# Six of a step's sixteen scans keep their states in PSUM, and the products by C are shared ten to six between GpSimd and VectorE

## The chip, the cores and the metric

The kernel runs on one core of one Trainium2 chip. The metric is the device time of one execution in microseconds (us). The kernel before took 2140.8 us, the median of three executions (2138.98 to 2144.34). Engines: PE is TensorE (PEld its weight loads), DVE is VectorE, ACT is ScalarE, POOL is GpSimd, SP issues most of the DMAs.

## What is computed

A batch of 16 sequences of 256 tokens with 128 features passes through four selective-scan (Mamba) layers, an output projection with a residual and a layer norm, and then a mixture of eight experts (top 2) with another residual and layer norm. The change touches the scan of the four layers alone:

```python
dA = jnp.exp(d_t[:, :, None] * A)
h = dA * h + (d_t * u_t)[:, :, None] * b_t[:, None, :]
y = jnp.einsum('bdn,bn->bd', h, c_t)
```

256 channels (d) have 16 states (n) each. The time axis is a first-order recurrence, which VectorE's tensor_tensor_scan carries out along the free dimension; the products by C and their sum over n follow.

## The kernel before, in words

**Steps, windows, slots.** The 4096 tokens are cut into 8 groups of 512 columns (two sequences each). A step is one layer of one group: 4 x 8 = 32 steps. Every engine's program runs through the same list of windows (`windows`, L290), one a step, and each window through 16 slots. In window s the scan of step s runs, and between its parts the engines prepare step s+1 (projections, softplus, the transposed products of delta and u), finish step s-1 (gate, output projection) and begin the norm of step s+2. The order on each engine is written out by hand in its `window` function; engines meet by semaphores alone.

**What a slot does.** 256 channels x 16 states are 4096 rows, 128 a tile. A slot is two such tiles (u = 0, 1) of 512 columns. m = slot // 4 counts four blocks of states; a block has four slots.
1. The outer products of B and delta u: 16 small instructions a block write the transposed inputs dbu_t[m % 2]; GpSimd makes 8 (`outer`, L455, lines L469 and L472), ScalarE 8 (`outer`, L630, L641). GpSimd's slots get 4, 2, 2 and 0 of them (POOL_SHARE). Those for the next step's first block lie in slots 13, 14 and 15 (POOL_FIRST); the wait for du_t and b_t that goes ahead of them stands in slot 12, where no outer product does, and in front of that slot's product.
2. TensorE transposes them into PSUM (`to_channels`, L1057, L1067), 8 transposes a slot, into dbu_ps[slot % 2]: two buffers of two banks each. They wait for the scan two slots back, which has read that buffer.
3. ScalarE makes the decays exp(delta A) (`exps`, L549, L563), up to four slots ahead of the scans.
4. VectorE scans (`scan`, L822, L829): inputs decay (SBUF) and dbu_ps (PSUM), states into ring[slot % 8] (SBUF).
5. The product by C, in place in the ring: VectorE for even slots, in the slot after (`times_c`, L834, L838), GpSimd for odd slots, in the slot after (`times_c`, L474, L478; that of slot 15 in slot 0 of the next window). Both operands are in SBUF. 8 products each.
6. TensorE sums over the states: `quad` (L1045, L1052), 4 slices of two slots at a time, into y_ps.

**Around it.** TensorE's window function sets the order of its work behind the transposes of a slot: in slots 0 and 1 a half convolution of the next step each (L1080), in slots 1 and 3 the last two quads of the step before, in slot 2 the z projection (L1090), which waits for ScalarE's silus (xc, L574) and is followed by ScalarE's sz (L579), in slot 4 a skip product (L1167), the dbc projection (L1097, copied by ScalarE at L587) and the mean square, in slot 6 the dt projection, in slot 9 the turned B and the output projection, in slot 11 the transposes of du (`turn_du`, L1145), from slot 5 on a quad in each odd slot. ScalarE's softplus ends with sp_l (L610) in its slot 8; VectorE finishes it in slot 8, behind the scan (L860, L864, L868 delta); GpSimd makes du = delta u in slot 10 (L488); TensorE transposes it; ScalarE copies it out as du_t in its slot 14 (L626); then GpSimd and ScalarE make the next step's first outer products. VectorE's gate (L844) multiplies sz by y_ps in slots 2 and 4. SP copies delta for the decays (d_rep) and brings C (c_rep) for the next step.

Semaphores that matter: scan_done counts scans (16 a step), hc_dve and hc_pool count the products (8 a step each), dbut_pool and dbut_act the outer products, quad_done the quads; a scan in an even slot waits until the quads have read the ring buffers that it and the next overwrite.

After the 32 windows the experts run for some 430 us, without scans; the change touches one wait at their start (`up`, L1270).

Of the kernel before, what the change touches and what calls it, by code (L numbers as in the profile page):

```python
# [21 lines left out]
STEPS = LAYERS * GROUPS  # L22
PAIRS = STEPS // 2
KT = DI // 128
# [9 lines left out]
SZ = 3  # L34
POOL_J = 2
EPS = 1e-5

# [28 lines left out]
def build_program(nc, xT, x_rows, norm_w, Win, conv_w, conv_b, Wx, Wdt, bdt, A_log, Dp, Wblk, Wout, bout,  # L66
                  gate_w, w1, w2, out):
    ctx = ExitStack()
    with ctx:
# [232 lines left out]
        def is_last(s):  # L302

            return has(s, 0) and not has(s, 1)

        def has(s, offset):

            return not isinstance(s, int) or 0 <= s + offset < STEPS
# [15 lines left out]
        def _(sp):  # L324
# [42 lines left out]
            def window(s, i, par):  # L367
# [32 lines left out]
                if is_last(s):  # L400
                    sp.wait_ge(skip_done, STEPS)
                    sp.wait_ge(hc_dve, SLOTS // 2 * (STEPS - 1))
                    sp.wait_ge(hc_pool, SLOTS // 2 * (STEPS - 1))
                    for e in range(EXPERTS):
                        sp.dma_start(w2_sb[e], w2[e, :, :].rearrange("(c p) d -> p c d", p=128))\
                            .then_inc(w2_loaded[e // half], 16)
# [22 lines left out]
        def _(pool):  # L429
# [44 lines left out]
            def times_c(s, i, par, slot):  # L474
                if slot == 1:
                    pool.wait_ge(c_loaded[par], 16 * (i + 1))
# [5 lines left out]
            def window(s, i, par):  # L482
                nxt = 1 - par
                for slot in range(SLOTS):
# [9 lines left out]
                    if slot == 0 and has(s, -1) and has(s, 0):  # L494
                        times_c(s - 1, i if par else i - 1, nxt, SLOTS - 1)
                    elif slot % 2 == 0 and slot and has(s, 0):
                        times_c(s, i, par, slot - 1)
# [23 lines left out]
        def _(act):  # L521
# [61 lines left out]
            def copy_dbc(s, par):  # L583
# [5 lines left out]

                wait(act, hc_dve, SLOTS // 2 * (s - 1))  # L590
                wait(act, hc_pool, SLOTS // 2 * (s - 1))
                act.dma_start(c_dram[par, :, :], dbc[RANK + NS:NBC, :]).then_inc(c_stored, 16)
# [198 lines left out]
        def _(dve):  # L791
# [30 lines left out]
            def scan(s, slot):  # L822
# [4 lines left out]
                if slot % 2 == 0:  # L827
                    wait(dve, quad_done, SLOTS // 2 * s + (slot - RING) // 2 + 1)
                nc.vector.tensor_tensor_scan(ring[slot % RING].rearrange("p u t -> p (u t)"),  # L829
                                             decay[slot % DEC].rearrange("p u a t -> p (u a t)"),  # L830
# [3 lines left out]
            def times_c(s, i, par, slot):  # L834
                if slot == 0:
                    dve.wait_ge(c_loaded[par], 16 * (i + 1))
                dve.wait_ge(scan_done, SLOTS * s + slot + 1)
                nc.vector.tensor_tensor(ring[slot % RING], ring[slot % RING],  # L838
                                        c_rep[par][:, slot // PRS, :].unsqueeze(1).broadcast_to([128, 2, TG]),
                                        ALU.mult).then_inc(hc_dve, 1)  # L840
# [5 lines left out]
            def window(s, i, par):  # L846
                for slot in range(SLOTS):
                    if has(s, 0):
                        scan(s, slot)
                        if slot % 2:  # L850
                            times_c(s, i, par, slot - 1)
                    if has(s, -1):
# [186 lines left out]
        def _(pe):  # L1039
# [5 lines left out]
            def quad(s, m, k):  # L1045

                extra = 1 if is_last(s) and m == M - 1 and k == KT - 1 else 0
                pe.wait_ge(hc_dve, SLOTS // 2 * s + 2 * m + k + 1 + extra)
                pe.wait_ge(hc_pool, SLOTS // 2 * s + 2 * m + k + 1 - extra)
                for j in range(Q):  # L1050
# [6 lines left out]
            def to_channels(s, slot):  # L1057

                m, p = slot // PRS, slot % PRS
                if p == 0:  # L1060
                    pe.wait_ge(dbut_pool, POOL_OUTER * (M * s + m + 1))
                    pe.wait_ge(dbut_act, ACT_OUTER * (M * s + m + 1))
                wait(pe, scan_done, SLOTS * s + slot - 1)
                for u in range(2):
# [205 lines left out]
            def up(g, par, e):  # L1270
# [3 lines left out]
                for c in range(FC):  # L1274
                    if is_first(g, e) and c % 2 == 0:

                        pe.wait_ge(scan_done, SLOTS * STEPS - 1 + c // 2)
                    n = FC * EXPERTS * g + FC * e + c
# [77 lines left out]
```

## Time and profile before

| | |
|---|---|
| median of three executions | 2140.8 us |
| the profiled execution, first to last instruction | 2143.5 us |
| TensorE busy, matmuls | 1877.8 us (88%) |
| VectorE busy | 1943.2 us (91%) |
| ScalarE busy | 1683.8 us (79%) |
| GpSimd busy | 1458.1 us (68%) |
| mean granted TensorE clock | 0.948 |

A core's own time is its span: the profiled execution is 2143.5 us long, 0.1% over the median. The last fifth of the span has no GpSimd work to speak of, so the shares say little; what a change in the scan phase is worth has to be read in one window.

### The profile page before, as it was taken

The page shows a single profiled execution, that of the slowest core. Times are in us where ns is not written, and L with a number is a line of the kernel's source. Part 1 is how long each engine was busy: PE and PEld are TensorE (multiplying, and loading weights), DVE is VectorE, ACT ScalarE, POOL GpSimd, SP SyncE. Part 2 cuts the span into 40 slices and gives each one's busy share as a digit, 9 for nine tenths or more (in the row PEclk, how much of TensorE's full clock was granted, in tenths as well). Part 3 has the DMA queues.
Part 4 walks back from the last instruction along what each step waited for, and adds up shares of the span by engine and source line. Part 5 has one row for each costly group of instructions (what it writes and reads, how often), then busy time and mean ns, then how long its engine had stood idle before and what let it go on. Part 6 is the DMA issues. An engine that isn't in the chain of part 4 may idle for free.

```text
span 2143.5 us, 34659 instructions
## 1 busy us (share of the span) xinstructions
PE 1877.8 (88%) x10816; PEld 1183.1 (55%) x10816; DVE 1943.2 (91%) x1826; ACT 1683.8 (79%) x3053; POOL 1458.1 (68%) x1364
## 2 busy tenths in 40 slices
PE   4788888888888888888888888888888799999998
PEld 1444444444444444444444445444444499989998
DVE  3799999999999999999999999999999987767775
ACT  4899999899999998989999999999999433333333
POOL 2688888888888888888888988888889600000000
PEclk9899999999999999999999999999999999999999
DMA  7323232323232323232333333332322200000000
GB/s 241 86 64 79 63 78 62 78 62 78 62 79 63 80 65 79 64 79 65 81 78 73 81 76 79 78 78 62 78 62 72 84 1 11 11 12 11 11 6 11
DMA packets 72786, 138.55 MB, mean 65 GB/s; under 512 B 13072, under 2 KB 31120, under 8 KB 68112
## 3 DMA queue, kind: packets, MB, share of 16 engines
q1 hardware_dynamic: 66320, 119.28, 22.7%
q10 hardware_dynamic: 6400, 18.42, 3.7%
q8 instruction: 39, 0.64, 0.1%
q14 instruction: 27, 0.22, 0.0%
HBM read 63.85 MB, written 7.74 MB: 33 GB/s over the span
## 4 chain that ended last, share of the span: by engine, by line
ACT 27%; PE 26%; POOL 26%; issue 13%; DVE 6%; ACTq 1%; SPq 1%; DMA 1%; POOLq 0%; DVEq 0%
POOL scan L478 12%; POOL scan L472 11%; PE y_ps L1291 11%; ACT decay L563 10%; PE dbu_ps L1266 8%; ACT scan L641 6%; DVE scan L829 3%; POOL scan L469 2%; PE dbu_ps L1067 2%; ACT sp_e L600 2%; ACT delta L601 2%; ACT sp_l L610 2%; PE y_ps L1052 2%; ACT sp_e L605 1%; ACT du_t L626 1%
## 5 line engine op out<-in xcount | busy, mean ns | idle before, releaser
L829 DVE TENSOR_TENSOR_SCAN scan<-decay,dbu_ps 128x1024 f32<-128x1024 f32 x512 | 1154.6, 2274 | 29.8 <-PE dbu_ps L1067 21.9
L1067 PE MATMUL dbu_ps<-ident,scan 128*128 128x128 f32 x4096 | 571.6, 286 | 220.7 <-DVE scan L829 195.9
L478 POOL TENSOR_TENSOR scan<-scan,c_rep 128x1024 f32<-128x1024 f32 x255 | 671.8, 2635 | 130.4 <-ACT du_t L626 66.5
L1067 PEld LDWEIGHTS dbu_ps<-ident,scan 128*128 128x128 f32 x4096 | 482.2, 147 | 500.1 <-DVE scan L829 259.3
L563 ACT ACTIVATE decay<-d_rep,a_cur 128x510 f32<-128x510 f32 x1024 | 668.0, 709 | 54.1 <-POOL scan L478 15.7
L472 POOL TENSOR_SCALAR scan<-du_t,b_t 128x256 f32<-128x256 f32 x896 | 594.8, 679 | 0.0
L641 ACT ACTIVATE scan<-du_t,b_t 128x256 f32<-128x256 f32 x1024 | 445.6, 494 | 1.2
L838 DVE TENSOR_TENSOR scan<-scan,c_rep 128x1024 f32<-128x1024 f32 x257 | 331.0, 1288 | 0.0
L766 ACT ACTIVATE decay<-dbu_ps 128x512 f32<-128x512 f32 x256 | 147.9, 597 | 205.2 <-PE dbu_ps L1266 183.1
L1052 PE MATMUL y_ps<-scan,sel 128*32 128x512 f32 x2048 | 299.8, 661 | 0.0
L1080 PE MATMUL pre_ps<-xn,w_pre 128*128 128x512 f32 x512 | 245.5, 603 | 5.2 <-DVE w_pre L818 5.2
L507 POOL TENSOR_TENSOR sp_e<-sp_e,bout_rep 128x512 f32<-128x512 f32 x8 | 11.2, 1399 | 277.1 <-DMA sp_e<-in_x_rows 277.1
L1266 PE MATMUL dbu_ps<-split_all 128*128 128x512 f32 x768 | 191.3, 400 | 5.8 <-DVE split_all L892 3.5
L1002 DVE TENSOR_TENSOR decay<-decay 128x512 f32<-128x512 f32 x256 | 163.6, 686 | 9.2 <-ACT decay L766 8.1
L1266 PEld LDWEIGHTS dbu_ps<-split_all 128*128 128x128 f32 x768 | 141.1, 190 | 35.2 <-issue 7.7
L989 DVE SCALAR_TENSOR_TENSOR xc<-y_ps,cw,xc 128x128 f32<-128x128 f32 x256 | 72.0, 344 | 95.4 <-PE y_ps L1291 95.4
L1080 PEld LDWEIGHTS pre_ps<-xn,w_pre 128*128 128x128 f32 x512 | 87.8, 191 | 97.4 <-issue 90.6
L488 POOL TENSOR_TENSOR sp_l<-delta,xc 128x1024 f32<-128x1024 f32 x32 | 75.2, 2351 | 81.2 <-DVE delta L868 81.2
L1291 PEld LDWEIGHTS y_ps<-w_pre,decay 128*128 128x128 f32 x1024 | 119.1, 192 | 3.6 <-issue 1.1
L1291 PE MATMUL y_ps<-w_pre,decay 128*128 128x128 f32 x1024 | 119.5, 275 | 0.2 <-DVE decay L1002 0.2
L1291 PEld LDWEIGHTS y_ps<-c_rep,decay 128*128 128x128 f32 x1024 | 118.0, 192 | 1.9
L1291 PE MATMUL y_ps<-c_rep,decay 128*128 128x128 f32 x1024 | 118.1, 275 | 0.0
(110 smaller groups left out, 1648.8 us busy)
## 6 DMA issues: line engine op xcount, KB each, us to landing
d_rep<-delta SPq DMA_DIRECT2D x496, 128.0 KB, 2.9
c_rep<-c_rows SPq DMA_DIRECT2D x32, 1024.0 KB
w_pre<-prepared_weights ACTq DMA_DIRECT2D x15, 866.0 KB, 13.0
prepared_weights<-scan SPq DMA_DIRECT2D x3, 1122.0 KB, 12.9
scan<-in_conv_w SPq DMA_DIRECT2D x4, 512.0 KB, 5.0
w_out<-prepared_weights SPq DMA_DIRECT2D x16, 128.0 KB, 12.5
sp_e<-in_x_rows SPq DMA_DIRECT2D x8, 256.0 KB, 3.2
d_rep<-in_w ACTq DMA_DIRECT2D x2, 1024.0 KB, 6.8
```

The source lines that it names most:

```text
L472: nc.gpsimd.tensor_scalar(dst, src, col, 1.0, ALU.mult, ALU.mult).then_inc(dbut_pool, 1)
L478: nc.gpsimd.tensor_tensor(ring[slot % RING], ring[slot % RING], c_rep[par][:, slot // PRS, :].unsqueeze(1).broadcast_to([128, 2, TG]), ALU ...
L563: last = nc.scalar.activation(decay[slot % DEC][:, u, :, 1:], src[:, :, 1:], ACT.Exp, scale=a_cur[:, b, m:m + 1])
L641: nc.scalar.activation(dbu_t[m % 2][:, j, :, q, :], du_t[par][:, j, :].rearrange("p (b c) -> p b c", b=UNITS), ACT.Copy, scale=b_t[par][:, ...
L829: nc.vector.tensor_tensor_scan(ring[slot % RING].rearrange("p u t -> p (u t)"), decay[slot % DEC].rearrange("p u a t -> p (u a t)"), dbu_p ...
L838: nc.vector.tensor_tensor(ring[slot % RING], ring[slot % RING], c_rep[par][:, slot // PRS, :].unsqueeze(1).broadcast_to([128, 2, TG]), ALU ...
L1002: nc.vector.tensor_tensor(hid[e % 2][:, c, :], hid[e % 2][:, c, :], hid[e % 2][:, c, :], ALU.mult).then_inc(h2_ready, 1)
L1052: last = nc.tensor.matmul(y_ps[k][CH * j:CH * j + CH, :], sel[:, :], ring[slot % RING][:, j % 2, :], start=False, stop=m == M - 1, skip_gr ...
L1067: last = nc.tensor.transpose(dbu_ps[slot % 2][:, u, 128 * j:128 * j + 128], dbu_t[m % 2][:, j, b, :, :].rearrange("p q c -> p (q c)"), ide ...
L1080: tap = nc.tensor.matmul(o, w_pre[:, c0:c0 + 128], xn[:, :, k:k + SEQ], start=k == 0, stop=k == KC - 1, skip_group_check=True)
L1266: last = nc.tensor.matmul(dst, left[l], right[r], start=start and n == 0, stop=stop and n == len(passes) - 1)
L1291: last = nc.tensor.matmul(moe_ps[e % 2][:, DM * j:DM * j + DM], hid[e % 2][:, c, 128 * j:128 * j + 128], w2_sb[e][:, c, :], start=c == 0, ...
```

## The change

DVE_SLOTS = (2, 4, 6, 8, 10, 14). In these six slots the scan writes its states over its own input in dbu_ps, and VectorE makes the product by C in the same slot, right behind the scan, from PSUM and c_rep into the ring. The other ten products (slots 0, 1, 3, 5, 7, 9, 11, 12, 13, 15) are GpSimd's, each in its slot after; those scans still write into the ring. In the last step VectorE also makes the product of slot 15, as before, but with the states in PSUM. The transposes of slot n+2 wait for VectorE's product n where n is one of the six, and for scan n elsewhere. The counts at the other waits are adapted.

```diff
+DVE_SLOTS = (2, 4, 6, 8, 10, 14)
+DVE_C = len(DVE_SLOTS)
+POOL_C = SLOTS - DVE_C
...
+        def by_vector(s, slot):
+
+            return slot in DVE_SLOTS or is_last(s) and slot == SLOTS - 1
+
+        def vector_products(s, slot):
+
+            return DVE_C * s + sum(by_vector(s, n) for n in range(slot + 1))
+
+        def pool_products(s, slot):
+
+            return POOL_C * s + sum(not by_vector(s, n) for n in range(slot + 1))
...
-                    sp.wait_ge(hc_dve, SLOTS // 2 * (STEPS - 1))
-                    sp.wait_ge(hc_pool, SLOTS // 2 * (STEPS - 1))
+                    sp.wait_ge(hc_dve, DVE_C * (STEPS - 1))
+                    sp.wait_ge(hc_pool, POOL_C * (STEPS - 1))
...
             def times_c(s, i, par, slot):
-                if slot == 1:
+                if slot == 0:
                     pool.wait_ge(c_loaded[par], 16 * (i + 1))
...
-                    elif slot % 2 == 0 and slot and has(s, 0):
+                    elif slot and has(s, 0) and not by_vector(s, slot - 1):
                         times_c(s, i, par, slot - 1)
...
-                wait(act, hc_dve, SLOTS // 2 * (s - 1))
-                wait(act, hc_pool, SLOTS // 2 * (s - 1))
+                wait(act, hc_dve, DVE_C * (s - 1))
+                wait(act, hc_pool, POOL_C * (s - 1))
...
-                nc.vector.tensor_tensor_scan(ring[slot % RING].rearrange("p u t -> p (u t)"),
+                states = dbu_ps[slot % 2][:, :, :] if by_vector(s, slot) else ring[slot % RING]
+                nc.vector.tensor_tensor_scan(states.rearrange("p u t -> p (u t)"),
...
-                if slot == 0:
+
+                if slot == DVE_SLOTS[0]:
                     dve.wait_ge(c_loaded[par], 16 * (i + 1))
                 dve.wait_ge(scan_done, SLOTS * s + slot + 1)
-                nc.vector.tensor_tensor(ring[slot % RING], ring[slot % RING],
+                nc.vector.tensor_tensor(ring[slot % RING], dbu_ps[slot % 2][:, :, :],
...
-                        if slot % 2:
-                            times_c(s, i, par, slot - 1)
+                        if slot in DVE_SLOTS:
+                            times_c(s, i, par, slot)
...
-                extra = 1 if is_last(s) and m == M - 1 and k == KT - 1 else 0
-                pe.wait_ge(hc_dve, SLOTS // 2 * s + 2 * m + k + 1 + extra)
-                pe.wait_ge(hc_pool, SLOTS // 2 * s + 2 * m + k + 1 - extra)
+                wait(pe, hc_dve, vector_products(s, PRS * m + 2 * k + 1))
+                wait(pe, hc_pool, pool_products(s, PRS * m + 2 * k + 1))
...
-                wait(pe, scan_done, SLOTS * s + slot - 1)
+                back, before = (s, slot - 2) if slot >= 2 else (s - 1, slot - 2 + SLOTS)
+                if has(s, -1) or slot >= 2:
+                    if by_vector(back, before):
+                        pe.wait_ge(hc_dve, vector_products(back, before))
+                    else:
+                        pe.wait_ge(scan_done, SLOTS * back + before + 1)
...
-                        pe.wait_ge(scan_done, SLOTS * STEPS - 1 + c // 2)
+                        last = SLOTS - 2 + c // 2
+                        if by_vector(STEPS - 1, last):
+                            pe.wait_ge(hc_dve, vector_products(STEPS - 1, last))
+                        else:
+                            pe.wait_ge(scan_done, SLOTS * (STEPS - 1) + last + 1)
```

## Rows read from the trace of the kernel before

**Rows 1.** The page: busy time of the engines; VectorE's product; the delta line, all windows

```profile
PE 1877.8 (88%) x10816; PEld 1183.1 (55%) x10816; DVE 1943.2 (91%) x1826; ACT 1683.8 (79%) x3053; POOL 1458.1 (68%) x1364
...
L838 DVE TENSOR_TENSOR scan<-scan,c_rep 128x1024 f32<-128x1024 f32 x257 | 331.0, 1288 | 0.0
...
L868 DVE TENSOR_TENSOR delta<-delta,sp_l x32: 1224/1225/1382, 40.8 to 1635.3; 128x1024 f32<-128x1024 f32 x32
```

**Rows 2.** Four stretches of one window: length; PE, PEld, DVE, ACT, POOL busy (instructions); clock; DMA

```profile
780.21:790.09 9.88, 9.88 (x52) 5.67 (x52) 9.87 (x7) 7.29 (x13) 9.88 (x10) 1.00 0.00 0
790.09:809.04 18.95, 18.59 (x105) 9.56 (x104) 17.88 (x11) 18.04 (x29) 17.38 (x18) 1.00 0.15 40
809.04:821.92 12.88, 8.16 (x50) 5.12 (x48) 12.78 (x8) 12.18 (x24) 8.19 (x6) 0.87 0.93 197
821.92:831.54 9.62, 7.71 (x42) 3.42 (x40) 9.62 (x6) 6.39 (x14) 9.46 (x11) 1.00 0.41 94
```

**Rows 3.** Timeline, TensorE's transposes 0 and 2, VectorE's scan 2 (start, length)

```profile
780.21 1.09 PE L1067 MATMUL dbu_ps<-ident,scan 128*128 128x128 f32 x8 [0.56 <-POOL scan L472]
...
786.54 1.09 PE L1067 MATMUL dbu_ps<-ident,scan 128*128 128x128 f32 x8
...
787.75 2.29 DVE L829 TENSOR_TENSOR_SCAN scan<-decay,dbu_ps 128x1024 f32<-128x1024 f32 x1
```

**Rows 4.** Waits of the whole run: us in total, times, longest

```profile
POOL scan L478 <- ACT du_t L626: 66.5, 31, 2.5
...
PE dbu_ps L1067 <- POOL scan L472: 20.8, 31, 2.8
```

**Rows 5.** Timeline of GpSimd behind du_t, in two windows, and TensorE's transposes 0'

```profile
770.10 2.92 POOL L478 TENSOR_TENSOR scan<-scan,c_rep 128x1024 f32<-128x1024 f32 x1 [1.65 <-ACT du_t L626]
...
822.08 2.37 POOL L478 TENSOR_TENSOR scan<-scan,c_rep 128x1024 f32<-128x1024 f32 x1 [2.43 <-ACT du_t L626]
...
824.39 0.62 POOL L469 TENSOR_TENSOR scan<-du_t,b_t 128x256 f32<-128x256 f32 x1
...
824.99 3.31 POOL L472 TENSOR_SCALAR scan<-du_t,b_t 128x256 f32<-128x256 f32 x5
...
831.68 1.09 PE L1067 MATMUL dbu_ps<-ident,scan 128*128 128x128 f32 x8 [0.81 <-POOL scan L472]
```

**Rows 6.** Timeline of VectorE beside it: product 12, scans 14 and 15, scans 0' and 1'

```profile
826.31 1.20 DVE L838 TENSOR_TENSOR scan<-scan,c_rep 128x1024 f32<-128x1024 f32 x1
827.42 4.45 DVE L829 TENSOR_TENSOR_SCAN scan<-decay,dbu_ps 128x1024 f32<-128x1024 f32 x2
...
833.13 4.55 DVE L829 TENSOR_TENSOR_SCAN scan<-decay,dbu_ps 128x1024 f32<-128x1024 f32 x2
```

**Rows 7.** Timeline of softplus on VectorE, of TensorE's transposes of du, of ScalarE's du_t

```profile
809.07 1.25 DVE L860 SCALAR_TENSOR_TENSOR sp_w<-sp_w,sp_e 128x1024 f32<-128x1024 f32 x1 [0.72 <-ACT sp_l L610]
810.36 1.38 DVE L864 SCALAR_TENSOR_TENSOR sp_l<-sp_l,sp_w 128x1024 f32<-128x1024 f32 x1
...
818.38 1.56 PE L1145 MATMUL pre_ps<-ident,sp_l 128*128 128x128 f32 x8
...
820.86 1.06 ACT L626 ACTIVATE du_t<-pre_ps 128x512 f32<-128x512 f32 x2
```

**Rows 8.** Timeline: a GpSimd product beside VectorE's, outer products beside a gate

```profile
845.79 3.25 POOL L478 TENSOR_TENSOR scan<-scan,c_rep 128x1024 f32<-128x1024 f32 x1 [0.35 <-DVE scan L829]
...
848.93 0.66 DVE L844 TENSOR_TENSOR sz<-sz,y_ps 128x512 f32 x1
...
849.02 1.84 POOL L472 TENSOR_SCALAR scan<-du_t,b_t 128x256 f32<-128x256 f32 x4
```

**Rows 9.** Timeline: TensorE's transposes 4, ScalarE's dbc copy, ScalarE's decays 0'

```profile
791.15 1.09 PE L1067 MATMUL dbu_ps<-ident,scan 128*128 128x128 f32 x8
...
794.99 0.59 ACT L587 ACTIVATE dbc<-pre_ps 96x512 f32<-96x512 f32 x1 [0.24 <-PE pre_ps L1097]
...
828.88 1.33 ACT L563 ACTIVATE decay<-d_rep,a_cur 128x510 f32<-128x510 f32 x2 [3.20 <-DMA d_rep<-delta]
```

## The prediction

> **What bounds the kernel now.** I read the page first, then cut one window of the scan phase at the points where one engine hands over to the next, and then read the timelines at those points. A window is one of the 32 steps (16 slots each); scan n, product n and transposes n are those of slot n, and a dash marks the next window. The delta row [rows 1] runs from 40.8 to 1635.3 us over 32 windows, so a window takes 51.4 us. VectorE is busy 91% of the span [rows 1], and in the four stretches of a whole window 9.87 + 17.88 + 12.78 + 9.62 = 50.1 of 51.3 us [rows 2]. That looks like a VectorE bound, and a change that takes two products away from VectorE looks like a gain.
>
> The same rows show a second loop that is just as long. It goes from the start of TensorE's transposes 0 to the start of transposes 0', in four legs that follow each other without a gap [rows 2]:
> - 9.88 us on TensorE: transposes 0, half a convolution, transposes 1, the other half, a quad, transposes 2, then the z projection; ScalarE's second sz ends the leg. TensorE is busy 9.88 of 9.88 us. VectorE's scan 2 starts at 787.75, when transposes 2 have just ended [rows 3].
> - 18.95 us on ScalarE, to the end of its sp_l; busy 18.04.
> - 12.88 us on ScalarE, to the end of the du_t copies; busy 12.18.
> - 9.62 us on GpSimd (busy 9.46), to the last outer product for m = 0, on which transposes 0' wait.
>
> The waits confirm the two hand-overs of the last leg: in 31 windows GpSimd's product waits for du_t, and in 31 TensorE's transposes wait for GpSimd's outer product [rows 4]. GpSimd is idle much of the window (busy 68% of the span [rows 1]), but this leg is full. So the loop through TensorE, ScalarE and GpSimd and the VectorE loop are within about half a microsecond of each other: transposes 0' started at 831.68 [rows 5], scan 0' at 833.13 [rows 6], 1.45 us later. Where a scan waits for its transposes it starts 1.2 us behind their start (786.54 and 787.75 [rows 3]), so GpSimd's leg has 0.2 us of slack to VectorE here.
>
> **The change, part by part.**
> 1. *VectorE loses products 0 and 12.* A product lasts 1.29 us in the mean [rows 1] and overlaps with what follows by 0.09 (826.31 + 1.20 against 827.42 [rows 6]), so 2 x 1.2 = 2.4 us of VectorE work per window go. A product now directly follows its own scan and waits for it: by the softplus pair, which also waits for its predecessor (809.07 + 1.25 to 810.36 [rows 7]), such a start comes 0.04 us after the end, where the product's successor overlapped by 0.09. That is 0.13 us six times, 0.8 us back. VectorE's work becomes 50.1 - 2.4 + 0.8 = 48.5 us.
> 2. *The lock between VectorE and GpSimd goes.* A GpSimd product beside a VectorE product of two SBUF operands takes 3.25 us in place of 2.36 [rows 5, 8]. Beside the gate (848.93, one operand in PSUM, one in SBUF) four outer products take 1.84 us, 0.46 each, undisturbed [rows 8]. The new product has exactly the gate's kinds of operands, so I take no block at all; the other bound is the old 1.0 us each. The Trainium skill, SBUF — State Buffer, section "SBUF: two separate sides", gives the same reason: VectorE with two SBUF inputs and GpSimd take one shared port pair exclusively; the trace agrees by the rows just named.
> 3. *GpSimd gains products 0 and 12.* Product 0 comes in GpSimd's slot 1, behind the last leg; the outer products behind it (m = 1, needed by transposes 4, 10.9 us after transposes 0 [rows 3, 9]) would be done after: outer products 2.0, product 15 2.3, two outers 0.9, product 0 2.3, two outers 0.9, together 8.4 us. It is hidden, with 2.5 us left. Product 12 comes in slot 13. GpSimd's slot 12 holds the wait for du_t, even though no outer product stands there, and product 11 behind it; then four outers, now product 12, two outers, product 13, two outers, and only then transposes 0' may start. So product 12 lies whole on the fourth leg: +2.32 us (a product's pitch, 822.08 to 824.39 [rows 5]). The leg without blocks is 0.16 + 2.32 + 0.60 + 5 x 0.46 + 2.32 + 2 x 0.46 = 8.6 us [rows 5, 8]; with product 12 it is 10.9. Before it was 9.62, because VectorE's product 12 at 826.31 [rows 6] stretched the five outers to 3.31; in the window ahead product 11 was hit too (2.92 us [rows 5]). Net: +1.3 us in the one kind, +0.9 in the other.
> 4. *Transposes n+2 now wait for product n where n is VectorE's.* TensorE starts transposes 4 at 791.15 [rows 9]. Scan 2 ends at 790.04 [rows 3], product 2 follows and ends 1.2 later, so transposes 4 start at about 791.35: +0.2. Queued behind them are the skip, the dbc projection and the mean square, and ScalarE already waits 0.24 for dbc [rows 9], so the 0.2 goes into the loop. At the other five the wait is covered: TensorE comes to the later transposes behind its own fillers, when the product is over on my walk of the window; product 14 releases transposes 0', which GpSimd holds longer.
> 5. *Softplus comes behind product 8.* VectorE now idles 0.72 us for sp_l there [rows 7]; the product takes 1.2, so delta comes about 0.4 later. du goes through GpSimd and TensorE's transposes back to ScalarE, which in this kind of window reaches du_t only at 820.86, 0.9 us after the transposes' end at 818.38 + 1.56 [rows 7]; in every other window (no DMA issue and self-wait on ScalarE) TensorE is last, and the 0.4 counts. Mean +0.2.
> 6. *Scans write in place into PSUM.* No row shows VectorE writing PSUM. Nearest is the gate, which reads there. I take no difference; if each of the six cost up to 0.1 us more, it would lie in the idle time of step 7. Below nothing I see no reason for a gain. A product from PSUM I take as 1.2, too. The Trainium skill, VectorE: DVE Perf Modes, section on the TRN2 errata, speaks against the change: a fixed 120 cycles for a PSUM source against 58, some 65 ns at its clock. The gate row (0.66 us for 512 elements) shows no such term. By the page product 2 would end 0.07 later and the loop be 0.07 longer, some 2 us in all.
> 7. *The sum.* 2.32 - 1.1 (blocks gone, mean of the two kinds) + 0.2 + 0.2 = +1.6 us per window; where d_rep comes late, as by 3.20 us at 828.88 [rows 9], the longer leg hides part of it, so I take +1.4. Over 31 windows that is +44 us. VectorE gets 48.5 us of work in a window of 52.9 and idles mostly before scans 0' and 2. The changed waits ahead of the c_rows store and ahead of the w2 loads are met long before; the first up projections of the second stage wait for a product in place of a scan, once, at most 1.2 us.
>
> The profiled execution took 2143.5 us, the median is 2140.8, 0.1% less; I add the 44 us to the median: **2185 us**. A measurement of this kernel tells about 0.3% (6.4 us) from no change.
>
> **The rivals.**
> - *VectorE was the true bound (faster).* If product 12 did not lengthen GpSimd's leg, because du_t comes early enough or the leg has more room than 0.2 us, the loop could fall to ScalarE's: its 51.3 less the 1.1 of blocks, plus 0.4, about 50.6, or -0.7 us x 31 = -22: 2119 us. It decides at a fourth leg under 9.3 us. For it speaks VectorE's 91%; against it that rows 4 count 31 windows of 31. Chance 0.08.
> - *Blocks stay, or PSUM is slow.* If the product on PSUM still locks GpSimd out, product 14 falls beside products 12 and 13 and adds 1.0 us per window: 2216 us. The same comes of in-place scans that are 1 us longer each (6 us on 48.5 pass the loop). The gate row speaks against the first; nothing shows the second. Chance 0.14.
> - *A draw.* GpSimd's leg grows by 0.9 only and steps 4 and 5 cost nothing, and late d_rep is hidden: +0.3 us or less a window, under 2150 us. Chance 0.08, half of it within 0.3%.
> - *My forecast:* 0.70.
>
> **The numbers.** Steps 4 and 5 at nothing and 0.9 for GpSimd give +28, 2169; step 5 whole in all windows and 1.3 everywhere give +59, 2200. I reach down to 2158 for part of the draw and up to 2216 for the lock. Faster 0.09, same 0.05, slower 0.86.
>
> **What would show it.** GpSimd's leg, du_t's end to the last outer for m = 0, near 10.9 us with product 12 at 2.36; outer products at 0.47 us and products at 2.36 everywhere outside softplus; VectorE's busy time down by about 80 us, and its idle time ahead of scans, put down to the transposes L1067, up by about 100. GpSimd's busy time falls although it has 64 products more in all. The forecast is wrong if scan 0' still starts behind VectorE's own work, if the first leg is no longer 9.9 us, or if the in-place scans exceed 2.4 us.

## The result, and the profile after

The kernel after takes 2224.51 us (median of 4 runs, 2223.39 to 2225.40), the kernel before 2141.61 us on the same chip (4 runs, 2138.98 to 2144.34). The ratio is 1.0381, 95% interval 1.0361 to 1.0402: slower by 83 us, where 44 us were forecast. The direction held, the size did not: 2224.5 lies above the range, which ended at 2216. The profiled execution took 2225.26 us, its span 2223.5.

From the page of the kernel after: busy time, share of the span and number of instructions of each engine; then the share of each engine in the chain that ended last; then the groups of instructions that answer to [rows 1, 6, 8] (busy time, mean ns of one | idle time ahead of them, and what ended it). Scans are now L845, VectorE's products L855, GpSimd's products L493 and outer products L487, the transposes L1088, the convolution L1101.

```profile
PE 1908.3 (86%) x10816; PEld 1185.6 (53%) x10816; DVE 1865.4 (84%) x1762; ACT 1681.5 (76%) x3053; POOL 1359.1 (61%) x1428
...
PE 36%; ACT 26%; issue 12%; POOL 9%; DVE 8%; ACTq 1%; DMA 0%; POOLq 0%; SPq 0%; DVEq 0%
...
L493 POOL TENSOR_TENSOR scan<-scan,c_rep 128x1024 f32<-128x1024 f32 x319 | 754.6, 2366 | 223.9 <-DVE scan L845 139.9
L845 DVE TENSOR_TENSOR_SCAN scan<-decay,dbu_ps 128x1024 f32<-128x1024 f32 x319 | 724.0, 2279 | 138.1 <-PE dbu_ps L1088 136.3
...
L845 DVE TENSOR_TENSOR_SCAN dbu_ps<-decay,dbu_ps 128x1024 f32<-128x1024 f32 x193 | 439.7, 2278 | 58.2 <-PE dbu_ps L1088 49.2
...
L487 POOL TENSOR_SCALAR scan<-du_t,b_t 128x256 f32<-128x256 f32 x896 | 417.8, 483 | 0.0
...
L1101 PE MATMUL pre_ps<-xn,w_pre 128*128 128x512 f32 x512 | 280.1, 676 | 6.0 <-DVE w_pre L833 5.7
L855 DVE TENSOR_TENSOR scan<-dbu_ps,c_rep 128x1024 f32<-128x1024 f32 x193 | 236.3, 1225 | 8.8
```

Most of the local prices are as forecast. VectorE's busy time fell by 77.8 us (about 80 were expected). A scan in place in PSUM costs 2278 ns, one into SBUF 2279; a product from PSUM costs 1225 ns. GpSimd's products are at 2366 ns and its outer products at 483, so the lock is gone, and GpSimd's busy time fell by 99 us although it has 64 products more. VectorE waits 185 us for the transposes (136.3 + 49.2), 164 more than before (21.9), where some 100 more were expected.

One line of this page is not as forecast: the 512 convolution matmuls take 280 us together, 35 more than before (245.5), though nothing in them was changed. The stretches of one window show why. As in [rows 2], a line is a stretch: its length, busy us of PE, PEld, DVE, ACT, POOL, the granted clock and the DMA. The first line is leg 1 of a window in which the clock did not fall; the second is the idle stretch ahead of the transposes 0 of another window, and the other four are legs 1 to 4 of that window.

```profile
921.51:931.39 9.88, 9.88 (x52) 5.67 (x52) 6.87 (x3) 6.34 (x11) 9.88 (x11) 1.00 0.00 0
...
1026.44:1028.51 2.07, 0.02 (x2) 0.01 (x1) 1.18 (x1) 2.07 (x6) 2.07 (x4) 1.00 0.00 0
1028.51:1040.08 11.57, 11.57 (x52) 6.53 (x52) 6.87 (x3) 6.30 (x11) 10.57 (x11) 0.85 0.00 0
1040.08:1059.33 19.25, 17.56 (x102) 8.99 (x101) 18.78 (x12) 18.03 (x29) 14.93 (x18) 1.00 0.15 37
1059.33:1072.22 12.89, 9.14 (x52) 5.62 (x51) 12.69 (x9) 12.18 (x24) 5.70 (x5) 0.87 0.95 194
1072.22:1083.19 10.97, 7.91 (x43) 3.51 (x41) 9.34 (x5) 10.29 (x21) 10.82 (x12) 1.00 0.36 89
```

Legs 2 to 4 are 19.25, 12.89 and 10.97 us; the working of the prediction had 19.15, 12.88 for this kind of window and 10.9. Leg 1 is 11.57 us in place of 9.88, with the same 52 matmuls, TensorE busy all through, at a granted clock of 0.85. Ahead of it TensorE had done 0.02 us of work in 2.07.

The timelines of TensorE and VectorE around three starts of leg 1 (start, length, in brackets the idle time ahead and what ended it). The first pair is the window in which the clock did not fall.

```profile
921.51 1.09 PE L1088 MATMUL dbu_ps<-ident,scan 128*128 128x128 f32 x8 [2.02 <-POOL scan L487]
922.44 1.88 PE L1101 MATMUL pre_ps<-xn,w_pre 128*128 128x512 f32 x4
...
1028.51 1.52 PE L1088 MATMUL dbu_ps<-ident,scan 128*128 128x128 f32 x8 [2.05 <-POOL scan L487]
1029.82 3.18 PE L1101 MATMUL pre_ps<-xn,w_pre 128*128 128x512 f32 x4
...
1083.32 1.71 PE L1088 MATMUL dbu_ps<-ident,scan 128*128 128x128 f32 x8 [2.89 <-POOL scan L487]
1084.83 2.98 PE L1101 MATMUL pre_ps<-xn,w_pre 128*128 128x512 f32 x4
1085.17 2.29 DVE L845 TENSOR_TENSOR_SCAN scan<-decay,dbu_ps 128x1024 f32<-128x1024 f32 x1 [3.58 <-PE dbu_ps L1088]
```

TensorE stands idle for 1.9 to 3.1 us ahead of transposes 0', 2.4 in the mean. Before it was 0.2 to 0.8 ([rows 3] and [rows 5] show 0.56 and 0.81). Of the 30 windows that follow another and have a whole leg 1, in 25 the granted clock then falls to its lower level, 1.2 GHz, at some point between 0.3 us before the start of the transposes and 1.3 us behind it, and leg 1 lasts 11.4 to 11.6 us; in five the clock stays at 2.4 GHz and leg 1 lasts 9.8 to 9.9. Four convolution matmuls take 3.18 us in the one case, 1.88 in the other. VectorE idles 3.58 us ahead of scan 0', for TensorE's transposes, which wait for GpSimd. The wait of the transposes for GpSimd's outer product, in us over the whole run, times and longest, against the second line of [rows 4]:

```profile
PE dbu_ps L1088 <- POOL scan L487: 77.0, 32, 4.4
```

It is 56 us longer than before, about 1.8 us a window.

GpSimd behind du_t, in the window whose legs stand above, against [rows 5]:

```profile
1072.37 2.38 POOL L493 TENSOR_TENSOR scan<-scan,c_rep 128x1024 f32<-128x1024 f32 x1 [3.13 <-ACT du_t L641]
1074.71 0.62 POOL L484 TENSOR_TENSOR scan<-du_t,b_t 128x256 f32<-128x256 f32 x1
1075.30 1.40 POOL L487 TENSOR_SCALAR scan<-du_t,b_t 128x256 f32<-128x256 f32 x3
1076.66 2.39 POOL L493 TENSOR_TENSOR scan<-scan,c_rep 128x1024 f32<-128x1024 f32 x1
1079.00 0.96 POOL L487 TENSOR_SCALAR scan<-du_t,b_t 128x256 f32<-128x256 f32 x2
1079.90 2.37 POOL L493 TENSOR_TENSOR scan<-scan,c_rep 128x1024 f32<-128x1024 f32 x1
1082.24 0.95 POOL L487 TENSOR_SCALAR scan<-du_t,b_t 128x256 f32<-128x256 f32 x2
```

The product at 1076.66 is the added one, product 12. Nothing is blocked any more, every duration is the short one, and the leg is still 1.2 us longer on the mean.

The account in us, as means over 25 windows in the middle of the scan phase (numbers 3 to 27, counted from 0). A window is its four legs and 0.14 us between the last outer product and transposes 0'.

| part of the window | before | after | forecast |
|---|---|---|---|
| leg 1, TensorE | 10.01 (9.88, but 11.6 in two, at full clock, d_rep late) | 11.34 (11.4 to 11.6, but 9.88 in three) | 9.88 |
| leg 2, ScalarE | 18.95 | 19.26 | 19.15 |
| leg 3, ScalarE | 12.6 | 12.5 | 12.8 |
| leg 4, GpSimd | 9.76 | 10.97 | 10.9 |
| window | 51.49 | 54.17 | 52.9 |

Legs 2 to 4 add 1.36 us together (+0.31, -0.16, +1.21), close to the forecast's 1.4. The other half of the loss, 1.33 us a window, came with leg 1.

### The profile page after: what moved, and what is told of

Read it like the earlier page. It is cut to its first block, busy times and chain, and to the rows that moved or that the text cites. A ratio compares the mean times of both kernels' runs of the same rounds, so it can differ in the third digit from the quotient of the medians.

```text
span 2223.5 us, 34532 instructions
## 1 busy us (share of the span) xinstructions
PE 1908.3 (86%) x10816; PEld 1185.6 (53%) x10816; DVE 1865.4 (84%) x1762; ACT 1681.5 (76%) x3053; POOL 1359.1 (61%) x1428
## 3 DMA queue, kind: packets, MB, share of 16 engines
q1 hardware_dynamic: 66320, 119.28, 21.9%
## 4 chain that ended last, share of the span: by engine, by line
PE 36%; ACT 26%; issue 12%; POOL 9%; DVE 8%; ACTq 1%; DMA 0%; POOLq 0%; SPq 0%; DVEq 0%
PE y_ps L1316 10%; ACT decay L578 10%; PE dbu_ps L1287 8%; ACT scan L656 6%; PE dbu_ps L1088 6%; PE pre_ps L1101 6%; POOL scan L487 4%; DVE dbu_ps L845 4%; POOL scan L493 4%; PE pre_ps L1118 2%; DVE scan L855 2%; PE y_ps L1068 2%; ACT sp_e L615 1%; ACT delta L616 1%; DVE scan L845 1%
## 5 line engine op out<-in xcount | busy, mean ns | idle before, releaser
L493 POOL TENSOR_TENSOR scan<-scan,c_rep 128x1024 f32<-128x1024 f32 x319 | 754.6, 2366 | 223.9 <-DVE scan L845 139.9
L845 DVE TENSOR_TENSOR_SCAN scan<-decay,dbu_ps 128x1024 f32<-128x1024 f32 x319 | 724.0, 2279 | 138.1 <-PE dbu_ps L1088 136.3
L1088 PE MATMUL dbu_ps<-ident,scan 128*128 128x128 f32 x4096 | 570.7, 284 | 274.0 <-DVE scan L845 164.2
L1088 PEld LDWEIGHTS dbu_ps<-ident,scan 128*128 128x128 f32 x4096 | 475.9, 145 | 571.6 <-DVE scan L845 251.8
L845 DVE TENSOR_TENSOR_SCAN dbu_ps<-decay,dbu_ps 128x1024 f32<-128x1024 f32 x193 | 439.7, 2278 | 58.2 <-PE dbu_ps L1088 49.2
L487 POOL TENSOR_SCALAR scan<-du_t,b_t 128x256 f32<-128x256 f32 x896 | 417.8, 483 | 0.0
L1101 PE MATMUL pre_ps<-xn,w_pre 128*128 128x512 f32 x512 | 280.1, 676 | 6.0 <-DVE w_pre L833 5.7
L855 DVE TENSOR_TENSOR scan<-dbu_ps,c_rep 128x1024 f32<-128x1024 f32 x193 | 236.3, 1225 | 8.8
L1101 PEld LDWEIGHTS pre_ps<-xn,w_pre 128*128 128x128 f32 x512 | 99.9, 216 | 111.9 <-issue 104.1
```

Of the source, the lines that this page charges most:

```text
L487: nc.gpsimd.tensor_scalar(dst, src, col, 1.0, ALU.mult, ALU.mult).then_inc(dbut_pool, 1)
L493: nc.gpsimd.tensor_tensor(ring[slot % RING], ring[slot % RING], c_rep[par][:, slot // PRS, :].unsqueeze(1).broadcast_to([128, 2, TG]), ALU ...
L845: nc.vector.tensor_tensor_scan(states.rearrange("p u t -> p (u t)"), decay[slot % DEC].rearrange("p u a t -> p (u a t)"), dbu_ps[slot % 2] ...
L855: nc.vector.tensor_tensor(ring[slot % RING], dbu_ps[slot % 2][:, :, :], c_rep[par][:, slot // PRS, :].unsqueeze(1).broadcast_to([128, 2, TG]),
L1088: last = nc.tensor.transpose(dbu_ps[slot % 2][:, u, 128 * j:128 * j + 128], dbu_t[m % 2][:, j, b, :, :].rearrange("p q c -> p (q c)"), ide ...
L1101: tap = nc.tensor.matmul(o, w_pre[:, c0:c0 + 128], xn[:, :, k:k + SEQ], start=k == 0, stop=k == KC - 1, skip_group_check=True)
```

## The experiments

The account that is tested has two parts: product 12 lies on GpSimd's leg and makes everything behind it 1.4 us later, as forecast; and the longer wait ahead of transposes 0' leaves TensorE without work, upon which its clock falls and leg 1 costs 1.7 us more. Against it stood that the states in PSUM are what costs, that ten products are too many for GpSimd wherever they lie, and that leg 1 waits for late products. Each expectation names the theories that its own run decides between, so "theory 2" isn't the same one everywhere. Each run was compared with the kernel before on the same chip; its median was 2144.06 us for runs 1 to 4, 2142.17 for runs 5 to 8 and 2143.49 for runs 9 to 11.

**1. Keep TensorE awake.** The kernel after, with 14 spare transposes of the identity into the bank that transposes 0' overwrite, done while TensorE waits for the outer products.

```
                 if slot == 0 and has(s, -1):
                     for n in range(14):
                         nc.tensor.transpose(dbu_ps[0][:, 0, 0:128], ident[:, :], ident[:, :])
                 if p == 0:
                     pe.wait_ge(dbut_pool, POOL_OUTER * (M * s + m + 1))
                     pe.wait_ge(dbut_act, ACT_OUTER * (M * s + m + 1))
```

> Changed kernel, but in slot 0 TensorE first makes 14 spare transposes of the identity into the dbu_ps buffer that it is about to overwrite, in the time in which it waits for GpSimd's outer products (2.1 to 2.9 us idle). Theory 1 (clock): the second half of the loss comes from TensorE's granted clock, which falls to its lower level behind that idle time in 27 of 31 windows and makes the first leg 11.56 us in place of 9.88. Then the leg is 9.88 in nearly all windows and the time 2224.5 - 27 x 1.7 = about 2179 us. Theory 2 (late product): the first leg is longer because a wait stands in it (a quad or a convolution waits for the later products 12 and 13); spare transposes change nothing, 2224 us or a little more.

Measured: 2188.10 us, ratio 1.0212 (1.0192 to 1.0231). The timeline of TensorE in one window of it, then the stretch of leg 1:

```profile
1005.89 1.69 PE L1084 MATMUL dbu_ps<-ident 128*128 128x128 f32 x14
...
1008.00 1.09 PE L1091 MATMUL dbu_ps<-ident,scan 128*128 128x128 f32 x8 [0.42 <-POOL scan L487]
1008.93 1.88 PE L1104 MATMUL pre_ps<-xn,w_pre 128*128 128x512 f32 x4
```

```profile
1008.00:1017.88 9.88, 9.88 (x52) 5.67 (x52) 6.87 (x3) 6.42 (x11) 9.88 (x11) 1.00 0.00 0
```

More work on TensorE makes the kernel 36 us faster. Transposes 0' still wait for the last outer product, leg 4 is still 10.97 us, but the clock is at its upper level in leg 1 of all 30 windows, leg 1 is 9.88 in all but two of the middle ones (10.24 and 10.72), and the window 52.89 us. What remains against the kernel before is 2188.10 - 2144.06 = 44.0 us. So the loss of 83 us has two parts, each by itself on the chip: some 36 us of clock, and 44 us of the longer loop (the three medians were taken apart, which leaves 2 or 3 us between the two parts and the whole). The time is 9 us above the expected 2179. In part the expectation counted 27 windows with a low clock, where the trace has 25. In part the edit has a cost of its own: it also puts the waits for the outer products behind the wait for the product two slots back, transposes 4 now start 0.24 us behind the end of VectorE's product 2 in place of 0.05, and leg 2 is 19.42 in place of 19.25. At 0.17 us a window that is some 5 us, so the clock's share is nearer 41 us and that of the longer loop nearer 39.

**2. Give product 12 back, and move product 8 to GpSimd instead.** The same split of six and ten, one constant changed.

```
-DVE_SLOTS = (2, 4, 6, 8, 10, 14)
+DVE_SLOTS = (2, 4, 6, 10, 12, 14)
```

> Changed kernel with products 2, 4, 6, 10, 12, 14 on VectorE (12 in place of 8), so product 12 leaves the part of GpSimd's work between du_t and the outer products for m = 0, and product 8 goes to GpSimd's slot 9, where it waits for delta anyway. Theory 1 (product 12 on GpSimd's leg is the cause, and the clock follows from it): GpSimd's leg 8.6 us in place of 10.97, first leg 9.88, window 50.4 us, time 2141 - 31 = about 2110 us, faster than both. Theory 2 (ten products are too many for GpSimd wherever they are): 2200 us or more. Theory 3 (VectorE holds the end of the window as soon as GpSimd does not): 2130 to 2145 us.

Measured: 2214.48 us, ratio 1.0327 (1.0310 to 1.0344); a miss. Leg 4 falls to 9.5 us (theory 1 wanted 8.6; in it GpSimd waits for scan 13, 0.68 us in one window), leg 1 is 9.82 at the full clock, and yet the window is 53.77. GpSimd's product 8 now falls beside softplus. The timeline of this kernel there, VectorE, GpSimd, TensorE:

```profile
625.45 3.43 DVE L877 SCALAR_TENSOR_TENSOR sp_w<-sp_w,sp_e 128x1024 f32<-128x1024 f32 x1 [0.73 <-ACT sp_l L625]
625.45 2.35 POOL L493 TENSOR_TENSOR scan<-scan,c_rep 128x1024 f32<-128x1024 f32 x1
...
633.66 1.97 PE L1088 MATMUL dbu_ps<-ident,scan 128*128 128x128 f32 x8 [5.44 <-DVE scan L845]
635.55 1.94 PE L1068 MATMUL y_ps<-scan,sel 128*32 128x512 f32 x8
```

Softplus's first instruction takes 3.43 us where it took 1.25 [rows 7]: this time it is VectorE that is held for as long as GpSimd's product lasts, and GpSimd that is undisturbed. Delta ends 6.0 us behind sp_l in place of 4.2 in the kernel after, TensorE idles 5.44 us ahead of transposes 11, which take 1.97 us for 1.09, and leg 3 becomes 14.3 us. Transposes 0' come another 0.9 us behind the last outer product. A new place of the lock and a low clock in another leg took back most of what legs 1 and 4 gained. The time also lies in the range of theory 2, ten products being too many anywhere. Run 7 decides between the two.

**3. The states back in SBUF, all else as after.**

```
-                states = dbu_ps[slot % 2][:, :, :] if by_vector(s, slot) else ring[slot % RING]
+                states = ring[slot % RING]
...
-                nc.vector.tensor_tensor(ring[slot % RING], dbu_ps[slot % 2][:, :, :],
+                nc.vector.tensor_tensor(ring[slot % RING], ring[slot % RING],
```

> Changed kernel with the states of all scans in the ring in SBUF, and VectorE's products from there; split, order and waits as in the changed kernel. Theory 1 (VectorE's two SBUF operands lock GpSimd out, PSUM states take that away): GpSimd's products beside VectorE's take 3.25 us again, product 14 adds 1.0 us to GpSimd's leg (12.0 us), the time is 2224 + 31 = about 2255 us. Theory 2 (PSUM states are themselves dear, in-place scans or products from PSUM are slower): the time falls below 2220 us.

Measured: 2352.25 us, ratio 1.0974 (1.0955 to 1.0992), 128 us slower than after. The groups of its page that answer to those above, and one of VectorE's products from its timeline:

```profile
L855 DVE TENSOR_TENSOR scan<-scan,c_rep 128x1024 f32<-128x1024 f32 x193 | 302.1, 1565 | 8.9
...
L487 POOL TENSOR_SCALAR scan<-du_t,b_t 128x256 f32<-128x256 f32 x896 | 567.0, 646 | 0.0
```

```profile
736.99 2.35 DVE L855 TENSOR_TENSOR scan<-scan,c_rep 128x1024 f32<-128x1024 f32 x1
```

The lock is back in both directions: outer products 646 ns in place of 483, VectorE's products 1565 in place of 1225, 33 of the 193 at 2.34 us or more. The direction is theory 1's; the size is four times what it said. Leg 4 is 13.03 us, so transposes 0' come later still, and TensorE idles 3.15 us ahead of them. Its clock is low from 0.9 us before their start to 5.9 us behind it, and leg 1 takes 12.78 us:

```profile
637.47:650.25 12.78, 12.78 (x52) 7.41 (x52) 6.86 (x3) 4.50 (x7) 10.59 (x11) 0.77 0.00 0
```

Theory 2 falls: putting the states into PSUM is the good part of this change. At this split it saves 128 us.

**4. Product 12 off the leg.** The kernel after, with products 12 and 13 behind the last outer products for m = 0, in GpSimd's slot 15.

```
+                    elif slot == SLOTS - 1 and has(s, 0):
+                        for late in (SLOTS - 4, SLOTS - 3):
+                            times_c(s, i, par, late)
-                    elif slot and has(s, 0) and not by_vector(s, slot - 1):
+                    elif slot and has(s, 0) and slot < SLOTS - 3 and not by_vector(s, slot - 1):
```

> Changed kernel, but GpSimd makes products 12 and 13 in its slot 15, behind the last outer products for m = 0. GpSimd's leg from du_t to the last of these becomes 6.3 us. Theory 1: the window is then set by VectorE up to product 14, which releases TensorE's transposes 0': about 49.3 to 50.5 us, 2075 to 2115 us, and the clock stays at its upper level ahead of them. Theory 2 (the late products hold the quads in TensorE's slots 1 and 3, or the outer products for m = 1 come too late for transposes 4): 2130 us or more.

Measured: 2134.57 us, ratio 0.9954 (0.9940 to 0.9968). Leg 4 is 6.30 us, the window 51.28. It is faster than the kernel before, but 20 us above the range of theory 1 and inside that of theory 2. The reasons that theory 2 gave are not the cause, though: leg 1 is 9.82 and leg 2 19.25 us in most windows, so neither quads nor transposes 4 are held. The timeline shows what comes next:

```profile
604.29 1.97 PE L1091 MATMUL dbu_ps<-ident,scan 128*128 128x128 f32 x8 [3.67 <-DVE scan L848]
...
608.05 1.97 PE L1169 MATMUL pre_ps<-ident,sp_l 128*128 128x128 f32 x8
...
611.16 4.46 DVE L848 TENSOR_TENSOR_SCAN scan<-decay,dbu_ps 128x1024 f32<-128x1024 f32 x2 [1.29 <-PE dbu_ps L1091]
```

Here it is transposes 11 that TensorE reaches too early: it waits 3.67 us for scan 9, which VectorE does behind softplus, and does them and the transposes of du at the low clock (1.97 us for 1.09). VectorE then waits 1.29 us ahead of scan 12.

**5. The same move in the kernel before.** Product 13 alone behind the outer products; states in SBUF, eight and eight.

```
-                    elif slot % 2 == 0 and slot and has(s, 0):
+                    elif slot % 2 == 0 and 0 < slot < SLOTS - 2 and has(s, 0):
                         times_c(s, i, par, slot - 1)
+                    elif slot == SLOTS - 1 and has(s, 0):
+                        times_c(s, i, par, SLOTS - 3)
```

> Kernel before, but GpSimd makes product 13 in its slot 15, behind the last outer products for m = 0, so its leg from du_t to these falls from 9.8 to about 7.4 us. Theory 1 (two loops of the same length before the change: GpSimd's and VectorE's): VectorE holds the window then, the gain is at most 0.3 us a window, 2135 to 2144 us, no difference that can be told. Theory 2 (GpSimd's loop alone was the bound and VectorE followed): 2144 - 31 x 2.3 = about 2072 us.

Measured: 2126.21 us, ratio 0.9920 (0.9891 to 0.9949), a gain of 16 us and 9 us under the range of theory 1. Leg 4 falls by 2.2 us to 7.52, the window only by 0.6, to 50.9. VectorE then idles 0.9 us in it (1.35 before), 0.64 of it for sp_l and 0.12 for transposes. That is the prediction's reading of the kernel before: two loops within about half a microsecond of each other. Even so, half a microsecond a window was open to a reordering of GpSimd's queue alone.

**6. The PSUM part alone.** Eight products stay on each engine, the even ones on VectorE from PSUM.

```
-DVE_SLOTS = (2, 4, 6, 8, 10, 14)
+DVE_SLOTS = (0, 2, 4, 6, 8, 10, 12, 14)
```

(and GpSimd's wait for the replicated C is back in slot 1, its first product.)

> The PSUM part of the change alone: products 0, 2, 4, ..., 14 on VectorE from states in PSUM, each right behind its scan, the other eight on GpSimd as before. Theory 1: GpSimd's leg is 8.6 us without blocks, VectorE's work 51 us a window is the bound, 2125 to 2150 us: the loss of the whole change comes from the two products more on GpSimd. Theory 2: the PSUM part itself costs (the transposes' wait for the product, the product's wait for its scan): 2165 us or more.

Measured: 2144.45 us, ratio 1.0015 (0.9995 to 1.0034): no difference. GpSimd's busy time is 1211.2 us against 1458.1 [rows 1], and leg 4 is 8.62 us in every other window, exactly the length the prediction worked out without blocks, and 9.2 in the rest. None of it reaches the end. From the waits of this kernel (us in total, times, longest):

```profile
PE dbu_ps L1088 <- DVE scan L855: 66.5, 61, 2.1
...
PE dbu_ps L1088 <- POOL scan L487: 5.0, 5, 1.4
```

Transposes 0' now start 0.7 to 0.9 us behind the last outer product (0.14 before), held by VectorE's product 14, whose bank they overwrite. The other loop is the longer one.

**7. Product 8 off softplus.** Run 2's split, with product 8 in GpSimd's slot 10, behind its product du.

```
+                    elif has(s, 0):
+                        for late in range(SLOTS - 1):
+                            if {8: 10}.get(late, late + 1) == slot and not by_vector(s, late):
+                                times_c(s, i, par, late)
```

> As a2_c12_vector (products 2, 4, 6, 10, 12, 14 on VectorE), but GpSimd makes product 8 in slot 10, behind du, in place of slot 9. In a2 VectorE's first softplus instruction took 3.43 us in place of 1.22, beside GpSimd's product 8. Theory 1 (the lock works both ways: VectorE's instruction with two SBUF operands waits until GpSimd's product has ended): softplus takes 1.22 again, delta comes 2 us earlier, TensorE stands still for less and its clock with it, about 2110 to 2145 us in place of 2214. Theory 2 (a2 was slow because of product 12's place on VectorE): still 2190 us or more.

Measured: 2141.81 us, ratio 0.9995 (0.9980 to 1.0011), 73 us less than run 2 by the place of one product. Delta ends 3.78 us behind sp_l. The lock of run 2 is shown by its removal, and ten products are not too many for GpSimd.

**8. Run 7 with product 13 late, too** (`{8: 10, 13: 15}` in the line above).

> As b3_c8_behind_du, and product 13 behind the last outer products for m = 0 (slot 15), so GpSimd's leg is 6.3 us. Theory 1 (GpSimd's leg no longer holds the window in b3, VectorE or TensorE does): the same as b3 within 0.5%. Theory 2 (GpSimd's leg still holds it): up to 2 us a window less than b3.

Measured: 2140.80 us, ratio 0.9997 (0.9985 to 1.0009). Leg 4 falls to 6.3 us and the time does not move: with product 12 on VectorE, GpSimd's leg no longer binds.

**9. Product 12 alone.** The kernel after, with product 0 on VectorE (and GpSimd's wait for C in slot 1, as in run 6).

```
-DVE_SLOTS = (2, 4, 6, 8, 10, 14)
+DVE_SLOTS = (0, 2, 4, 6, 8, 10, 14)
```

> One of the two products that GpSimd gained alone: VectorE makes 0, 2, 4, 6, 8, 10, 14 from PSUM, GpSimd keeps product 12. Theory 1 (product 12 on GpSimd's leg does all the harm): leg 10.9 us, clock lower in the first leg in most windows, 2215 to 2230 us, as the whole change. Theory 2 (the number of GpSimd's products does it, half of it each): about 2180 us.

Measured: 2227.48 us, ratio 1.0398 (1.0381 to 1.0415); leg 4 is 10.96 us, the window 54.03, the clock is low in 23 of 30 legs 1. Against run 6 that is +83 us for product 12, the whole loss of the change.

**10. Product 0 alone.** The kernel after, with product 12 on VectorE.

```
-DVE_SLOTS = (2, 4, 6, 8, 10, 14)
+DVE_SLOTS = (2, 4, 6, 8, 10, 12, 14)
```

> The other alone: VectorE makes 2, 4, 6, 8, 10, 12, 14 from PSUM, GpSimd gains product 0. Theory 1 (product 0 lies outside GpSimd's leg and costs nothing): leg 8.6 to 9.2 us, as b2_psum8, 2135 to 2150 us. Theory 2 (half of the harm): about 2180 us.

Measured: median 2152.71 us, ratio 1.0054 (1.0036 to 1.0073), 3 us above the expected range. The profiled execution took 2141.85, with a window of 51.20 us and leg 4 at 8.63 and 9.12; the others took 2152 to 2157. In the profile product 0 costs nothing, as forecast, and the whole change, which has it, has no larger ratio than run 9, which has it not (1.0381 and 1.0398). The half per cent of the other executions of run 10 has no trace and stays open.

**11. Run 4 with TensorE kept awake ahead of transposes 11.** While it waits for scan 9, TensorE adds twelve products of a zero matrix to y_ps, which changes nothing in it.

```
                 if slot == 11 and has(s, 1):
                     for n in range(12):
                         nc.tensor.matmul(y_ps[0][0:CH, 0:128], zeros[:, :], ident[:, :], start=False, stop=False,
...
```

> As a4_late12_13 (the changed kernel with products 12 and 13 behind the outer products), and in slot 11 TensorE adds twelve times zero to y_ps while it waits for scan 9 (about 4 us idle in a4; its clock then falls to the lower level, the transposes 11 take 1.97 us, the quad 1.94 and the transposes of du 1.97, and VectorE waits 1.3 us for transposes 12). Theory 1 (that lower clock holds the window in a4): VectorE's 1.3 us go, 2134 - 31 x 1.2 = about 2097 us. Theory 2 (something else holds it, or the spare work is too short to keep the clock): 2125 us or more.

Measured: 2111.98 us, ratio 0.9853 (0.9837 to 0.9870). Its timeline against that of run 4 (the 12 spare products show as 24 matmuls):

```profile
797.52 2.81 PE L1086 MATMUL y_ps<-ident,zeros 128*32 128x128 f32 x24
...
801.26 1.09 PE L1097 MATMUL dbu_ps<-ident,scan 128*128 128x128 f32 x8 [0.93 <-DVE scan L850]
...
803.28 1.09 PE L1175 MATMUL pre_ps<-ident,sp_l 128*128 128x128 f32 x8
```

Both groups of transposes are back at 1.09 us, the window is 50.67 us, and the kernel is 1.5% faster than the kernel before. It was expected at 2097; in the windows of 51.3 to 51.9 us, where d_rep comes late, leg 1 lasts 11.6 to 12.0. So a faster kernel with this change in it exists. In it products 12 and 13 are off GpSimd's last leg, and TensorE is given something to do in a wait. Whether the change itself has a part in the gain is not shown: run 5 gained 0.8% by moving one product in the kernel before, and spare work in that kernel was not tried.

## Why the prediction was right in direction and short in size

**The step that failed is step 7, the sum, with leg 1 held at 9.88 us.** Step 3 made leg 4 longer, from which it follows that TensorE waits longer ahead of transposes 0', and the prediction booked that wait as idle time that costs nothing beyond itself. The list of what would prove the forecast wrong named this very number ("if the first leg is no longer 9.9 us"), but no rival had it. The wait went from 0.2-0.8 to 1.9-3.1 us, the granted clock fell behind it in 25 of 30 windows, and leg 1 became 1.68 us longer there: 25 x 1.68 = 42 us by the trace; 36 us by run 1, whose edit cost some 5 itself. With the term added the sum is 2185 plus 36 to 42, 2221 to 2227, and 2224.5 was measured. The trace of before held a warning: in the third stretch of [rows 2] the clock is 0.87, and transposes there take 1.56 us [rows 7].

Step by step:
- *Two loops of equal length: right.* Run 5 took 2.2 us from GpSimd's leg and gained 0.6 a window before VectorE's loop held it.
- *Step 1, VectorE's work falls by 1.6 us a window: right* within what the trace tells (busy time -77.8 us in 32 windows is 2.4 a window, which is two products; the 0.8 of self-waits is idle time and not in it). The self-wait itself is there: a product starts at 1078.17, 0.03 us behind the end of its scan (1075.87 + 2.27).
- *Step 2, the lock goes, no block at all: right.* 2366 and 483 ns, and 8.62 us for the leg in every other window of run 6, where 8.6 was worked out. Run 3 is the counter-proof.
- *Step 3, product 12 lies whole on leg 4, product 0 is hidden: right.* 10.97 us against 10.9; run 9 has the whole loss with product 12 alone, run 10's profile none with product 0 alone (its median has 0.5%, unexplained).
- *Step 4, +0.2 us for the wait of transposes 4: right in kind.* Leg 2 grew by 0.3.
- *Step 5, +0.2 us for softplus behind product 8: wrong.* Delta ends 4.22 us behind sp_l against 3.98, so it is 0.24 later, but leg 3 is 12.5 us against 12.6: the lateness did not reach du_t. With step 4 this makes the sum 0.26 us a window too high.
- *Step 6, nothing for PSUM: right.* 2278 against 2279 ns for the scan. The term of some 65 ns for a product from PSUM, an estimate worked out from the Trainium skill, VectorE: DVE Perf Modes, section on the TRN2 errata, doesn't show: all 193 products from PSUM take 1.22 or 1.23 us, and the shortest of run 3, from SBUF and in the same place, takes 1.22, too.
- *The sum without the clock: right within 5 us.* Run 1 leaves 44.0 us where 44 was forecast. That the two agree to the last digit is luck: some 5 us of the 44.0 are the cost of run 1's own edit, and the 0.26 that steps 4 and 5 had too much is about what the forecast took off for a late d_rep.

Of the rivals, the draw fell with leg 4 at +1.2 us and leg 2 at +0.3, and "VectorE was the true bound" fell, as transposes 0' wait for GpSimd's outer products 32 times after as well. "Blocks stay, or PSUM is slow" had a time near the measured one (2216) for a reason that the trace contradicts: products at 2366 ns, scans at 2278. (Its second reason was also mispriced: 6 us on 48.5 exceed 52.9 by 1.6 a window, which is 50 us and not 31.) Had the measured time alone been looked at, this wrong reason would have seemed confirmed.

## What to carry to other kernels

A longer wait of an engine is not only its own length. Where TensorE has dense work behind the wait, price that work at both levels of its clock, taken from rows of the same trace, and let the forecast's range reach the second. And before a product is handed to the engine with the lowest busy share, look at which leg of the loop its slot lies on: here product 12 cost 83 us in slot 13, and with products 12 and 13 in slot 15, behind the outer products that others wait for, the kernel was 0.5% faster than before. The kernel before with product 13 alone in that place was 0.8% faster (run 5), so try the reordering by itself first.

## What was not expected of the hardware

- *The lock works in both directions.* In the kernel before it was GpSimd that was held for long (3.25 us for 2.36); VectorE's products never took more than 1.57 us for 1.20. In run 2 VectorE was: 3.43 us for a softplus instruction of 1.25, with GpSimd's product at its full speed beside it, both from 625.45 on. What decides which of the two is held was not tried.
- *An idle engine made slower by idling, a busier one faster.* 14 spare transposes (1.69 us of work per window) made the kernel 36 us faster, 12 spare products of zero (2.81 us) some 22 us.
- *The clock does not fall each time.* After waits of 2.02 to 2.05 us it fell at 1028.51 and did not at 921.51. The spared windows are numbers 1, 8, 16, 24 and 30. Between window 8 and window 16 the fall comes later and later, with small steps back, from 0.3 us before the start of transposes 0' to 1.3 us behind it; then comes the spared window. What sets this pattern was not tried.
- *One change, two sizes of loss.* Run 3 lost 128 us more than the kernel after, where the blocks alone were worth some 31 by the expectation. Leg 4 grew by 2.1 us (one block of 1.0 was expected), leg 3 by 0.35, and leg 1 by 1.4 (12.77 us against 11.34 in the mean), as the wait ahead of it was longer and the clock low for longer behind it.
